# Reordering ScalarE and GpSimd inside the GNN step of a GNN + mixture-of-experts kernel

## What is computed

```python
out1 = jax.ops.segment_sum(edge_attr, col, num_segments=n)
cnt  = jax.ops.segment_sum(ones, col, num_segments=n)
out2 = where(cnt > 0, jax.ops.segment_max(edge_attr, col, num_segments=n), 0)
out3 = out1 / jnp.maximum(cnt, 1.0)
h = jnp.concatenate([x, out1, out2, out3, u[batch]], axis=1)   # x is layernormed
h = jax.nn.relu(h @ W1 + b1) @ W2 + b2
x1 = x_raw + (h + x)
x2 = layernorm(x1)          # goes to a router, 2 of 16 experts, and a last layernorm
```

## Time and profile before

| what | value |
|---|---|
| median of 3 runs | 1422.58 us (1421.58 to 1425.25) |
| the profiled execution | 1423.21 us, its span 1421.5 us |
| busy share of the span | PE 85%, DVE 60%, POOL 56%, ACT 45% |
| chain that ended last | PE 54%, DVE 33%, DMA 4%, issue 4%, POOL 2%, ACT 1% |

### The profile page before, as it was taken

The page is one execution under the profiler, slowest core; times in us unless marked ns, Lnnn a source line. Parts: engine busy times, 40 slices in busy tenths (PEclk is TensorE's granted clock), DMA queues, the critical chain, the costliest instruction groups (busy, mean ns, idle before and its releaser), DMA issues.

```text
span 1421.5 us, 28692 instructions
## 1 busy us (share of the span) xinstructions
PE 1201.3 (85%) x6677; PEld 1015.0 (71%) x6678; DVE 848.0 (60%) x3007; ACT 645.1 (45%) x1969; POOL 795.2 (56%) x1060
## 2 busy tenths in 40 slices
PE   2004998998998999999998254999999999999798
PEld 1003887887887788788887144999999999998343
DVE  5999999999999899000000695344444344443796
ACT  5853555656656556566563000332323232323453
POOL 4874565665665566666751001676766777765122
PEclk7556999999999999999999577999999999999555
DMA  9976677676676656611110823122221222222883
GB/s 314 300 227 246 232 268 268 265 276 262 258 281 260 230 186 236 196 45 42 58 34 30 278 85 133 62 69 74 69 71 63 75 69 71 69 72 58 297 284 102
DMA packets 87468, 231.48 MB, mean 163 GB/s; under 512 B 22145, under 2 KB 34819, under 8 KB 87285
## 3 DMA queue, kind: packets, MB, share of 16 engines
q1 hardware_dynamic: 50401, 167.53, 32.5%
q0 software_dynamic: 26048, 43.47, 10.5%
q10 hardware_dynamic: 10964, 19.96, 4.0%
HBM read 116.42 MB, written 114.25 MB: 162 GB/s over the span
## 4 chain that ended last, share of the span: by engine, by line
PE 54%; DVE 33%; DMA 4%; issue 4%; POOL 2%; ACT 1%; DVEq 1%; SPq 0%; POOLq 0%; ACTq 0%
PE ps L1061 14%; PE ps L1069 14%; DVE mem L1142 12%; DVE mem L1146 12%; PE ps L983 5%; PE ps L969 5%; PE ps L971 5%; PE ps L1089 3%; PE ps L1091 3%; PE ps L1048 2%; DVE mem L1162 2%; DVE mem L1283 1%; DMA mem<-piece_carry,mem 1%; DMA mem<-in_edge_attr_dram 1%; DVE mem L1167 1%
## 5 line engine op out<-in xcount | busy, mean ns | idle before, releaser
L879 ACT ACTIVATE mem<-ps,mem 128x128 f32<-128x128 f32 x452 | 128.8, 368 | 374.8 <-PE ps L1061 374.8
L969 PE MATMUL ps<-mem 128*128 128x250 f32 x800 | 214.1, 391 | 27.2 <-ACT mem L769 25.7
L1061 PEld LDWEIGHTS ps<-mem 128*128 128x128 f32 x1808 | 221.8, 194 | 5.7
L1061 PE MATMUL ps<-mem 128*128 128x128 f32 x1808 | 222.2, 277 | 0.0
L1069 PE MATMUL ps<-mem 128*128 x904 | 213.8, 379 | 0.4 <-issue 0.4
L1142 DVE TENSOR_TENSOR_SCAN mem<-ps,mem 128x80 f32<-128x80 f32 x960 | 207.9, 303 | 0.3
L971 PE MATMUL ps<-mem 128*128 128x250 f32 x800 | 208.1, 383 | 0.0
L1146 DVE TENSOR_TENSOR_SCAN mem<-ps,mem 128x80 f32<-128x80 f32 x960 | 207.8, 308 | 0.0
L621 POOL DMA_INDIRECT expert_rows<-mem x113 | 138.2, 1223 | 113.3 <-DVE mem L1317 66.0
L969 PEld LDWEIGHTS ps<-mem 128*128 128x128 f32 x800 | 156.2, 198 | 47.5 <-ACT mem L769 27.4
L983 PE MATMUL ps<-mem 128*125 128x256 f32 x800 | 180.9, 379 | 0.7 <-ACT mem L769 0.7
(11 more groups left out here) (206 smaller groups left out, 1785.6 us busy)
## 6 DMA issues: line engine op xcount, KB each, us to landing
run_sum<-mem SPq DMA_DIRECT2D x40, 960.0 KB
run_max<-mem SPq DMA_DIRECT2D x40, 960.0 KB, 7.6
mem<-in_edge_attr_dram SPq DMA_DIRECT2D x36, 960.0 KB, 10.3
mem<-in_L_ffn_w_dram SPq DMA_DIRECT2D x32, 512.0 KB, 9.7
mem<-expert_rows SPq DMA_DIRECT2D x22, 512.0 KB, 6.0
x_rows<-mem ACTq DMA_DIRECT2D x25, 256.0 KB, 2.0
x_normed<-mem ACTq DMA_DIRECT2D x25, 256.0 KB, 2.8
mem<-in_x_dram ACTq DMA_DIRECT2D x24, 256.0 KB, 7.8
```

The costliest lines, as they stand in the source:

```text
L879: ins = act.activation(hT[b][:, c, :], bank(2 + b, c * P, (c + 1) * P), ACT.Relu, bias=eb1c[:, bass.ds(e, 1), c])
L969: pe.matmul(h, W1x[:, c, hc * P:(hc + 1) * P], XT[b][:, c, :], start=(c == 0), stop=False)
L1061: ins = pe.matmul(bank(2 + b, f * P, (f + 1) * P), w1now[b][:, c, f * P:(f + 1) * P], XgT[b][:, c, :], start=(c == 0), stop=(c == DC - 1))
```

## The change

ACT: `moments2(i-1)`'s first part (mean) moves ahead of `relu(i,0)`; `carry_in(i+1)` moves from ahead of `relu(i,0)` to behind `take_logits(i-2)`; `mask_rows` is split, and its XN part, now `node_part`, comes ahead of the wait for the join, with a semaphore of its own (`masked`) for the NB part; `turn` on PE waits for both. POOL: `norm1(i+1)` moves ahead of `cut(i+1)`, and `gather(i+2)` moves from behind `norm2(i-1)` to ahead of it. No instruction is added or taken away apart from one semaphore wait on PE. Code of after stands 3 to 8 lines further down in the file, so `relu`'s L769 is L772 there, `moments2`'s L778 and L783 are L781 and L786, XN's L755 is L748, and the mask's L749 to L751 are L755 to L757.

```diff
                 residual(i, g, b)
                 if more:
+                    norm1(i + 1)
                     cut(*after(i, g, b))
-                    norm1(i + 1)
                     join(*after(i, g, b))
+                if not isinstance(i, int) or i + 2 < MACROS:
+                    gather(*after(i, g, b, 2))
                 if norm:
                     norm2(i - 1)
-                if not isinstance(i, int) or i + 2 < MACROS:
-                    gather(*after(i, g, b, 2))
...
+            def node_part(i, g, b):
+                act.wait_ge(rstd1_ready, i + 1)
+                for a in range(2):
+                    ins = act.activation(XN[b][:, a, :], XR[b][0:NT, a, :], ACT.Identity, bias=nmr_1[:, a:a + 1], scale=rstd_1[:, a:a + 1])
+                ins.then_inc(node_rows, 1)
...
             def mask_rows(i, g, b):
                 act.wait_ge(joined, i + 2)
...
-                act.wait_ge(rstd1_ready, i + 1)
-                for a in range(2):
-                    ins = act.activation(XN[b][:, a, :], XR[b][0:NT, a, :], ACT.Identity, bias=nmr_1[:, a:a + 1], scale=rstd_1[:, a:a + 1])
-                ins.then_inc(node_rows, 1)
+                ins.then_inc(masked, 1)
...
                     moments1(*after(i, g, b), 1)
-                    carry_in(*after(i, g, b))
+                if norm:
+                    moments2(i - 1, 0)
                 relu(i, 0)
                 if logit:
                     take_logits(i - 2)
+                if more:
+                    carry_in(*after(i, g, b))
                 if norm:
-                    moments2(i - 1, 0)
                     moments2(i - 1, 1)
                 if not isinstance(i, int) or i + 2 < MACROS:
                     act.wait_ge(residual_ready, 2 * i + 2)
                     load_x(i + 2, b)
                 if more:
+                    node_part(*after(i, g, b))
                     mask_rows(*after(i, g, b))
                 relu(i, 1)
...
             def turn(i, g, b):
                 pe.wait_ge(node_rows, i + 1)
+                pe.wait_ge(masked, i + 1)
```

More of the change, by code:

```diff
@@ L324, in gnn_moe_kernel @@
         pick_step = sem("pick_step")
-        ix_copied, carried, joined, node_rows = sem("ix_copied"), sem("carried"), sem("joined"), sem("node_rows")
+        ix_copied, carried, joined, node_rows, masked = sem("ix_copied"), sem("carried"), sem("joined"), sem("node_rows"), sem("masked")
         xr_got = [sem(f"xr_got{i}") for i in range(2)]
@@ L750, in mask_rows @@
                     act.activation(NB[b][:, a, 2 * EF:2 * P], RAW[b][:, a, 0, 0:EF - REST], ACT.Identity, scale=rch[:, j])
-                    act.activation(NB[b][:, a, 2 * P:3 * P].rearrange("p (n r) -> p n r", n=QUAD), spread(RAW[b][:, a, 0, EF - REST:EF], 1, QUAD),
+                    ins = act.activation(NB[b][:, a, 2 * P:3 * P].rearrange("p (n r) -> p n r", n=QUAD), spread(RAW[b][:, a, 0, EF - REST:EF], 1, QUAD),
                                    ACT.Identity, scale=rch[:, j])
-                act.wait_ge(rstd1_ready, i + 1)
-                for a in range(2):
-                    ins = act.activation(XN[b][:, a, :], XR[b][0:NT, a, :], ACT.Identity, bias=nmr_1[:, a:a + 1], scale=rstd_1[:, a:a + 1])
-                ins.then_inc(node_rows, 1)
+                ins.then_inc(masked, 1)
             def take_turned(i, g, b):
@@ L852, in _ @@
             carry_in(0, 0, 0)
+            node_part(0, 0, 0)
             mask_rows(0, 0, 0)
```

## The result

The changed kernel takes 1596.86 us (median of 4 runs, 1596.41 to 1598.26) against 1423.35 us: 12.2% slower, ratio 1.122 with a 95% interval of 1.1201 to 1.124. Forecast were 1605 us and a range of 1555 to 1650 us. The span of the profiled execution grew by 175.1 us, from 1421.5 to 1596.6 us.

A forecast was written before the change was run, and what follows sets the result against it. PE was taken to bound the GNN stage. Span 1421.5 + 222 (gathers ahead of the second power) - 40 (stalls gone) = 1603.5, with 1.7 us around the span 1605 us; range 1555 to 1650 us.

The forecast's parts named there:

- Part 1: ACT, `relu` ahead of the carry: a late gather no longer holds `relu(i,0)`; 40 us (36 to 42) gone.
- Part 2: PE at `turn(i+1)`: later carry, join and mask cost 0.4 us a step, covered in nearly all steps by Part 3.
- Part 3: PE at `turn_x2`: `norm2` behind the gathers, waits of 7 us or more, 10.1 us a step, 222 us over 22 steps.
- The slow spell: PE's work behind each new gap: 3.9 to 6.2 us at 0.50 clock lose 2.0 to 3.1 us, taken as 2.6.
- (a): Rival: the second power is in time at `turn_x2`, only the late gathers' stalls go; 1392 us; 3%.
- (b): Rival: TensorE's clock holds in the new gaps; a step is 7.5 us longer, 1548 us; 4%.
- (c): Rival: TensorE's clock does not come back within a step, PE needs 48.8 us for it; 1920 us; 3%.

The follow-up runs named there:

- experiment 2: The kernel before with only the gathers moved ahead of the second power on POOL, ACT untouched: 1526.34 us, ratio 1.0737.
- Experiment 4: The changed kernel with both parts of `moments2` ahead of `relu(i,0)` on ACT and `norm2` between `cut` and `join` on POOL: 1393.34 us, ratio 0.9788.
- Experiment 5: The kernel of Experiment 1 with three indirect gathers a step instead of six: 1375.67 us, ratio 0.9673.
- Experiment 1: The changed kernel with the gathers put back behind the second power, ACT's reordering and `norm1` ahead of `cut` kept: 1420.19 us, ratio 0.9982.
- experiment 3: The changed kernel with three indirect gathers a step instead of six, only the first of two tiles gathered: 1474.41 us, ratio 1.0375.

## Why the prediction was right

**Part 1, the stalls behind `relu`: right.** 40 us were forecast as gone, 39.8 are by the account above. That it is ACT's order which frees them was not shown by the changed kernel alone, since the earlier gathers of experiment 2 do the same. Experiment 4 shows ACT's part at work: its last gather is out at T+25.9 in the mean, no earlier than in the kernel before, and no late gather stalls `relu(i,0)` in it. Experiment 5 does not separate the two, since half the gathers may end the late landings by themselves; ACT's old order with half the gathers was not run.

**Part 2, the mask: smaller.** 0.4 us were forecast for PE at `turn(i+1)`, 0.1 came (0.07 us in the steps of the loop). Half of the difference is a slip in adding: T+11.4 and the four terms behind it make T+16.2 for the mask and not T+16.4. The rest is ACT's links from `relu` to the mask, each up to 0.1 us shorter than its row; the mask ended at T+16.0. As forecast nothing hangs on it, since x2 sets the step.

**Part 3, the gathers ahead of the power: right, in two terms that missed in opposite ways.** The block from the join's end to the last issue's end took 11.3 us in the mean of the 22 steps against 11.5 forecast (10.3 in step 1 to 12.0 in step 22, 11.7 in the step shown). The chain from `norm2` to `turn_x2` is 3.40 us (824.75 to 828.15), not 2.70: I had taken it from the last step, which is written out; in the loop the power's instructions wait 0.39 and 0.27 us between each other and not 0.18, and `write_x2` starts 0.41 us behind `norm2` and not 0.11. Step 1 of the changed kernel, written out as well, has 0.18, 0.18 and 0.14 us there. The gap's end came at T+28.42 in the mean, not T+28.0. The slow spell behind the gap costs 34.10 - 28.42 - 3.89 = 1.8 us, not 2.6. That term was the mis-sized one: 22 x 0.8 = 18 us too much, of which the chain gave back 9. Together they come to 9 us too much, and 8 lie between 1605 and 1597: the two misses partly cancelled, which is luck. The range's low edge had 2.0 us for it, from the same rows of spells behind shorter gaps; 1.8 is outside even that.

**The rivals.** (a) would have shown `norm2` beside the gathers; it starts 0.06 us behind the last issue. (b): the clock does fall, to 0.79 in the mean over the gap and 0.65 in the spell. (c): it is back at full at the next T; the first matmul group of the next step takes 1.01 us as in the earlier trace rows. PE did not go on with layer 2 at the waiting transposes either: L991's second half starts after L1003.

**What I had not asked.** I took the 40 us for a gain of ACT's reordering that the gathers' move then drowned. Experiment 1 says that it would not have been one by itself: 1420 us where this term alone stood for 1383. POOL's round closes almost without a gap in the kernel before already, `add_rows` 0.01 us behind the last gather and in steps 3 to 23 never more than 0.6 us behind it except after a stalled step, so a link that becomes later by more than that lengthens it. The price of one edit held only beside the other.

## What to carry to other kernels

When a block of issues is moved ahead in an in-order queue, cost the small instruction that it passes by what waits on that: 1.8 us of power arithmetic behind 11.3 us of issues opened a 7.6 us gap on the busiest engine in every step. Before ordering such a queue by urgency, look for its idle time; the power fitted into a wait that was there anyway, and of the orders tried here with all six gathers only that one was faster than the kernel before (2.1%). And check the round of the feeding engine against the step: at 24.4 us a step and 16.2 us busy POOL looked idle, and its chain of waits still took 25.4 us once one link was later.

## What the runs showed of the hardware

Gaps of TensorE between 2.6 and 3.6 us sometimes lowered the clock and sometimes did not: two neighbouring steps in experiment 3 have 1.00 and 0.94, and the length alone does not sort them, for a step with a gap of 3.43 us kept 1.00 (662.67 to 690.84 us) and one with 3.02 us had 0.94 (455.08 to 484.55 us). With gaps of 7.6 us the steps of the changed kernel came out very even (33.95 to 34.44 us in steps 2 to 22), with about 1.8 us lost each time (1.4 to 2.1), less than the 2.0 to 3.1 us behind the shorter, irregular gaps of the kernel before. It is not the length of the gap that makes it less: in experiment 2, gaps of 3.8 to 5.0 us at the same place in the step cost 1.5 to 1.7 us each. The gaps of the kernel before lie elsewhere, in the second half of layer 1, and come in some steps only. Whether that is the reason I do not know; no run here varied the moment of the return by itself.
